# Two gated convolutions: the first one's input in three shifted copies with rows of 56, blocks of 7 slots

## The reference

```
def qconv_cg(x, w, theta):
    base = cin // 4
    yp = conv3x3(x[:, :base], w[:, :base])
    yr = conv3x3(x[:, base:], w[:, base:])
    d = sigmoid(2.0 * (yp - theta))
    return yp + d * yr
h = relu(bn(qconv_cg(x, w_a, theta_a), ...))
h = bn(qconv_cg(h, w_b, theta_b), ...)
return relu(x + h)
```

## Time and profile before

| | us |
|---|---|
| median of 3 runs (434.37 to 434.45) | 434.44 |
| the profiled execution, its own time | 433.95 |
| its span, first to last instruction | 432.0 |
| TensorE busy | 425.4 |
| VectorE busy | 246.4 |
| ScalarE busy | 198.7 |
| GpSimd busy | 30.2 |

### The profile page before, as it was taken

How to read it: one execution, slowest core, us unless ns; L and a number is a source line. 1 busy time by engine, 2 the same in 40 slices (tenths; PEclk the granted TensorE clock), 3 DMA queues, 4 the chain that set the end, 5 groups by cost and what they waited for, 6 DMA issues and landing times.

```text
span 432.0 us, 17302 instructions
## 1 busy us (share of the span) xinstructions
PE 425.4 (98%) x7808; PEld 423.3 (98%) x7808; DVE 246.4 (57%) x423; ACT 198.7 (46%) x337; POOL 30.2 (7%) x81
## 2 busy tenths in 40 slices
PE   9999999999999999999999999999999999999994
PEld 8999999999999999999999999999999999999994
DVE  6766644753764663575375375366357367436535
ACT  5755534534544553553453453354345345433333
POOL 6041000000000100000000000021000000000001
PEclk9999999999999999999999999999999999999998
DMA  8445116341615110520523161151622321012044
GB/s 161 92 80 98 28 26 124 66 85 27 125 25 101 25 28 2 101 51 5 122 61 79 37 124 29 26 123 26 123 49 59 69 51 43 9 27 50 4 97 94
DMA packets 120074, 27.57 MB, mean 64 GB/s; under 512 B 119488, under 2 KB 120000, under 8 KB 120000
## 3 DMA queue, kind: packets, MB, share of 16 engines
q1 hardware_dynamic: 116944, 25.82, 29.2%
q10 hardware_dynamic: 2736, 0.63, 0.7%
q0 software_dynamic: 320, 0.00, 0.0%
HBM read 13.60 MB, written 12.85 MB: 61 GB/s over the span
## 4 chain that ended last, share of the span: by engine, by line
PE 98%; DVE 1%; issue 0%; ACT 0%; DVEq 0%
PE acc L523 96%; PE acc L477 1%; DVE mix L828 0%; DVE rows_out L876 0%; DVE rows_out L873 0%; PE acc L550 0%; ACT mix L664 0%; DVE rows_out L918 0%; DVEq L832 0%; ACT rows_out L689 0%; DVEq L827 0%
## 5 line engine op out<-in xcount | busy, mean ns | idle before, releaser
L523 PE MATMUL acc<-x_lo,w_hi 32*128 32x456 f32 (+1 forms) x1392 | 251.0, 358 | 0.0
L523 PE MATMUL acc<-x_hi,w_lo 32*128 32x456 f32 (+1 forms) x1392 | 250.7, 358 | 0.0
L523 PE MATMUL acc<-x_hi,w_hi 32*128 32x456 f32 (+1 forms) x1392 | 250.3, 358 | 0.0
L523 PE MATMUL acc<-h_hi,w_lo 32*128 32x512 f32 x1152 | 243.9, 390 | 0.0
L523 PE MATMUL acc<-h_lo,w_hi 32*128 32x512 f32 x1152 | 243.4, 389 | 0.0
L523 PE MATMUL acc<-h_hi,w_hi 32*128 32x512 f32 x1152 | 243.1, 389 | 0.0
L523 PEld LDWEIGHTS acc<-x_lo,w_hi 32*128 32x128 f32 x1392 | 211.5, 183 | 0.1
L523 PEld LDWEIGHTS acc<-x_hi,w_hi 32*128 32x128 f32 x1392 | 211.3, 183 | 0.1
L523 PEld LDWEIGHTS acc<-x_hi,w_lo 32*128 32x128 f32 x1392 | 211.2, 183 | 0.1
L523 PEld LDWEIGHTS acc<-h_lo,w_hi 32*128 32x128 f32 x1152 | 184.2, 183 | 0.0
L523 PEld LDWEIGHTS acc<-h_hi,w_lo 32*128 32x128 f32 x1152 | 183.9, 183 | 0.1
(11 more groups left out here) (77 smaller groups left out, 156.2 us busy)
## 6 DMA issues: line engine op xcount, KB each, us to landing
out_dram<-rows_out SPq DMA_DIRECT2D x95, 126.0 KB, 2.5
x<-in_x_dram SPq DMA_DIRECT2D x28, 392.0 KB, 5.4
x<-in_x_dram SPq DMA_DIRECT2D x5, 98.0 KB, 3.6
x_edge<-in_x_dram SPq DMA_DIRECT2D x4, 112.0 KB, 4.0
out_dram<-rows_out SPq DMA_DIRECT2D x3, 112.0 KB, 2.8
x<-in_x_dram SPq DMA_DIRECT2D x1, 294.0 KB, 4.2
x<-in_x_dram SPq DMA_DIRECT2D x1, 280.0 KB, 4.9
x<-in_x_dram ACTq DMA_DIRECT2D x2, 98.0 KB, 3.8
```

What stands on the lines that cost most here:

```text
L523: return pe.matmul(sums(bank, blk), w[g * ROWS:(g + 1) * ROWS, tap], moving(blk, part, c, dx, g), start=(u == 0 and (alone or g == bank_gr ...
```

## The change

From image 2 on (the third), `x_hi` and `x_lo` hold each image in three copies, one for each tap dx, with rows of 56 and no zero between them: the middle copy is the image, the others are shifted by a column to either side, with a zero in the column that the shift leaves free. A product of dx reads the copy of dx, k x 56 columns: 392 for a block of 7. Images 0 and 1 keep the padded form. All a blocks have 7 slots, four to an image, and the blocks of 4 + 4 are gone.

```diff
-BLK, BLK_B = 8, 9
-SHORT, SHORT_PAIRS = 7, 2
+BLK, BLK_B = 7, 9
+PADDED = 2
+EDGE = 8
+LAST_IMGS, LAST_SIZES = 2, (7, 7, 7, 6)
...
-XH_IMGS, X_IMGS, H_IMGS, MIX, Z_RING, OUT_RING = 4, 5, 4, 4, 4, 4
+XH_IMGS, X_IMGS, H_IMGS, MIX, Z_RING, OUT_RING = 2, 4, 4, 4, 4, 4
...
-        x_hi = sb("x_hi", [P, XH_IMGS, 1 + XS * PITCH + 1], F32R)
+        x_hi = sb("x_hi", [P, XH_IMGS, TAPS * XS * W], F32R)
...
-        natural = sb("natural", [P, 5, HALF_NAT])
+        natural = rows_out[:, 0:2].rearrange("p r n -> p (r n)")[:, 0:5 * HALF_NAT].rearrange(
+            "p (z n) -> p z n", z=5)
...
+                    if tripled(blk):
+                        at = (dx * XS + s + c) * W
+                        return tile[rows, img % XH_IMGS, at:at + k * W]
...
+                            if tripled(blk) and a_slots[n][1] == 0 and a_slots[n][0] < PADDED + XH_IMGS:
+                                pe.wait_ge(shifts_zero, a_slots[n][0] - PADDED + 1)
...
+                nc.scalar.activation(shifted_chunk(x_hi, n, 1), x_chunk(n), ACT.Copy).then_inc(xhi_ready, 1)
+                for dx in (0, 2):
+                    to, source = shifted_parts(shifted_chunk(x_hi, n, dx), x_chunk(n), dx)
+                    nc.scalar.activation(to, source, ACT.Copy).then_inc(xhi_ready, 1)
...
+                dve.wait_ge(xhi_ready, his_done(n) - 2)
+                middle = shifted_chunk(x_lo, n, 1)
+                nc.vector.tensor_tensor(middle, x_chunk(n), shifted_chunk(x_hi, n, 1).bitcast(F32),
                                         ALU.subtract).then_inc(xlo_ready, 1)
+                dve.wait_ge(xlo_ready, los_done(n) - 2)
+                for dx in (0, 2):
+                    to, source = shifted_parts(shifted_chunk(x_lo, n, dx), middle, dx)
+                    nc.vector.tensor_copy(to, source).then_inc(xlo_ready, 1)
...
+                if first < XH_IMGS * ROUND:
+                    zero_shifts(first // ROUND)
```

More of the change, by code:

```diff
@@ L47, in gated_conv_pair_kernel @@
     PITCH = W + 1
[L48 removed]
+    SHORT = BLK
     HRING = H_IMGS * SLOTS
[L50 to L63, removed]
[L64 to L67 removed]
+    assert BLK_B * PITCH - 1 <= BANK and SLOTS == 4 * BLK == 3 * BLK_B + 1 and B % EDGE == 0
+    assert PADDED == XH_IMGS and sum(LAST_SIZES) == SLOTS - 1
+    a_slots = [(img, t, BLK) for img in range(B) for t in range(0, SLOTS, BLK)]
+    NA = len(a_slots)
+    a_of = {(img, t): n for n, (img, first, k) in enumerate(a_slots) for t in range(first, first + k)}
+    NE = B // EDGE
+    b_slots, b_last = [], []
+    for img in range(B):
+        s0 = 1
+        for k in LAST_SIZES if img >= B - LAST_IMGS else (BLK_B,) * 3:
+            b_slots.append((img, s0, k))
+            s0 += k
+        b_last.append(len(b_slots) - 1)
     second = []
[L70 to L72 removed]
+    for m, (img, s0, k) in enumerate(b_slots):
+        second.append(("b", m))
+        if m == b_last[EDGE]:
             second.append(("e", 0))
[L75 to L79 removed]
+    second.append(("e", 1))
     def a_needed(blk):
@@ L127, in slots_of, with tripled @@
         kind, n = blk
-        return BLK_B if kind == "b" else EDGE if kind == "e" else sum(k for img, t, k in a_slots[n])
+        return EDGE if kind == "e" else (a_slots if kind == "a" else b_slots)[n][2]
+    def tripled(blk):
+        return blk[0] == "a" and a_slots[blk[1]][0] >= PADDED
     def leading(blk):
@@ L137, in residual_done, with splits, his_done, los_done @@
     def residual_done(img):
-        return second_of["b", 3 * img + 2] + 1
+        return second_of["b", b_last[img]] + 1
     IN_BANK = (TOTAL - 3, TOTAL - 2)
     BY_TWO = len(second) - 2
[L148 to L159, removed]
+    edge_sources = [n for n, (img, t, k) in enumerate(a_slots) if t == 0 or t + k == SLOTS]
+    chunks = [(img, t + 1 if t else 0, t + k + 1) for img, t, k in a_slots]
+    def splits(n):
+        return TAPS if tripled(("a", n)) else 1
+    def his_done(n):
+        return sum(splits(m) for m in range(1, n + 1))
+    def los_done(n):
+        return sum(splits(m) for m in range(n + 1))
     with ExitStack() as ctx:
@@ L612, in split_hi @@
             def split_hi(n):
-                if chunks[n] is None:
-                    return
                 img, s0, s1 = chunks[n]
```

116 lines of the change are left out of this document (56 added, 60 removed).

## The result

The changed kernel takes 441.42 us (median of four runs, 441.26 to 441.67), the kernel before beside it 434.4 us (433.82 to 434.45): a ratio of 1.0165, interval 1.0153 to 1.0178. It is 1.6% **slower**. The forecast was 431.5 us, and its range ended at 434.0.

What follows compares the result with a forecast made beforehand. TensorE was taken as the bound, the time being one row group's sum of products. 2.5 us from columns and products plus 0.4 at the end gave 2.9 off 434.44: 431.5 us, range 430.9 to 434.0.

Steps and rivals of the forecast that it cites:

- The price of a column: TensorE products: 0.445 ns a column, the cost beside columns falling with width; rounds of two 392 and two 512 take 14.82 us.
- Rival 1: TensorE products: constant 18.3 ns each beside columns, so 433.8 us, no difference that can be told; chance 0.13.
- Rival 3: TensorE weight loads: 183 ns sets a product's least time, so 392 and 342 win nothing; 435.1 us; chance 0.05.
- Columns and products, the sum: TensorE visits after the first 8: 391.68 us falls to 389.17, from 6,912 fewer columns and 144 more products.
- my own paragraph on the splits: ScalarE and VectorE splitting x: up to nine splits a round, in five rounds, fit the slack; nothing lost.
- The gain of 2.5 us: TensorE's main term: time saved by narrower columns, net of the added products, 2.5 us.
- Splitting x: Three roundings on ScalarE, one subtraction and two copies on VectorE per chunk: 112 more instructions on each, costing nothing.
- The limit of 10.5 us: After a round's start, TensorE needs the bank back at 10.5 us; with nine splits ScalarE's affine copy ends at 10.0.
- The load of x: Loading images with four of x held instead of five: image 4 lands 5.4 us later, still before its split; nothing lost.
- The end: After the last product: smaller final blocks shorten VectorE's last work, gaining 0.4 us (0.2 to 0.5).

Runs made afterwards that it cites:

- whole rounds with ScalarE in time: Changed kernel with blocks reordered into rounds a, b, a, b plus four rounds of four a blocks, ScalarE's splits ahead of each round's last ReLU: 431.78 us.
- with the written order freed: The same reordered kernel with early ScalarE splits, its products also written by when each row group would be free: 430.99 us.
- the run with the end alone: Changed kernel's order, but from place 104 the remaining first blocks are taken at once, a63 at place 106 instead of 108: 439.20 us.

## Why the prediction was wrong

- **The price of a column: right.** 14.81 us a round against 14.82, in the rounds that it was read from. Rival 1 (15.0 or more, 18.3 ns a product beside its columns) falls: 392 alone goes at 179.0 ns, 15.7 over columns/2.4. The about 60 cycles a matmul of the Trainium skill, TensorEngine Tiling (Array Packing), "Instruction Overhead" (an estimate of 25 ns at 2.4 GHz), do not agree with this 15.7 either. Rival 3 falls too: visits of 342 columns that no other group holds go at 157.8 ns a product, below the 183 ns of a weight load.
- **Columns and products, the sum: wrong, and this is the step that failed.** I priced each visit by its own width and called the sum of one group the time. I took 21 rounds of a, b, a, b for granted without laying out the new order, which has four a blocks to three b, though my own paragraph on the splits counts five rounds with three a blocks. In the ragged rounds a group with 392 columns is tied to another group's 512. The sum was 389.2 us for the visits from 7 on; the changed kernel took 399.5. In whole rounds with ScalarE in time it is 390.0, and with the written order freed 388.8: the sum was that of a kernel whose groups are not tied. The gain of 2.5 us was also too large by the yardstick above: there the new widths and numbers of products are worth 388.0 - 386.7 = 1.3 us (1.6 with 232.0 ns for 512). The kernel before has only 3.7 us over its columns: its order is a, b, a, b in most rounds, and a 456 product stands 23 ns under one of 512 where a 392 product stands 51 under.
- **Splitting x: right.** Two of ScalarE's splits take 0.84 us as before, VectorE's copy 380 ns where 390 to 560 was the bound, and in a round with nine splits the z ends 221.98 - 212.21 = 9.8 us after the round's start (10.0 forecast), with no stand of TensorE:

```profile
212.21 0.68 ACT L673 ACTIVATE mix<-acc,gate_bias 128x504 f32<-128x504 f32 x1 [2.56 <-PE acc L526]
...
220.84 0.57 ACT L673 ACTIVATE mix<-acc,gate_bias 128x392 f32<-128x392 f32 x1
221.31 0.67 ACT L678 ACTIVATE z<-acc,shift,inv 128x392 f32<-128x392 f32 x1
...
L826 DVE CAST x_lo<-x_lo 128x385 fp32r<-128x385 f32 x84 | 28.5, 380 | 1.4
```

  The limit of 10.5 us fits as well: 9.8 passes, 11.2 made TensorE stand. My closing sentence, that a time above 434 us would mean copies that cost TensorE something, was wrong: without them the time is the same.
- **The load of x: right.** No product waits for a load in the rounds.
- **The end: half.** Behind the last product 0.5 us were won (0.4 forecast). But I looked only behind the last product and not at what the last second blocks wait for: a63 at place 108 costs 2.2 us (the run with the end alone).

The rivals were all about the price of single operations. None asked whether four groups with different blocks can each go at their own pace, though TURNS, OFFSET and the one queue were in the text.

## What to carry over

Where several row groups of TensorE are fed from one queue, add up the time of the queue and not only of each group: a change that makes the groups' products more unequal (392 beside 512 in place of 456) needs an order in which every group has the same mix in the same places of each round (the same mix in other places, b, a, b, a behind a, b, a, b, was 3.6 us slower), or a queue written by when each group is free. After a change in the number of blocks, lay out the whole new order, above all the last blocks, before pricing it. A page that shows a full TensorE does not show that: compare the starts of products of one width in two places.

## What the hardware showed that I had not expected

- TensorE takes the row groups' products nearly in the order in which they are written. Numbering them in that order, a product in the changed kernel's trace starts at most 11 places ahead of the oldest that has not started. In one visit a group with 392 columns would win 18 x 51 ns = 0.9 us on one with 512, four steps of four products, 16 places.
- The Trainium skill, TensorE: Matmul & The Clock Gate, in "The mechanism", says that matmuls start and end strictly in program order. The trace agrees in part: strictly in order, the rounds a, b, a, b, in which some group always has a 512, would take 72 x 230 ns = 16.6 us, and they take 14.81; the order holds, but with a lead of up to 11 places. The Trainium skill, TensorEngine Tiling (Array Packing), "Key Properties", says that the tiles work independently; by the products shown here they are so only within that lead.
- A wait at the head of that queue stops all four groups: with no slack at the bank there were 0.28 us without a start every 7.5 us, and six rounds a, b, a, b took 90.5 us in place of the 88.7 with one product of slack.
- After a stand of 3.4 us the granted clock was 1.2 GHz in the 5.3 us shown (x64 products recorded, where 2.4 GHz gave x201 in 9.9 us), so the stand cost nearly twice its length.
